# Mask on small PE tiles, norm turns on the full array, ten value moves for sixteen, and new engine orders in a fused attention stack

## The reference

```python
for i in range(DEPTH):                       # 6 layers
    x = attn_layer(shift_tokens(x), Wqkv[i], q_scale[i], k_scale[i], Wo[i]) + x
    x = ffn_layer(shift_tokens(x), ln_g[i], ln_b[i], W1[i], b1[i], W2[i], b2[i]) + x
# attn_layer: 16 heads of 64, windows of 32 tokens
q, k = l2norm(q) * qs, l2norm(k) * ksc       # then rotary with scales
mask = (it < jb) | (it > jb + w) | (jb == -1)    # a query sees 64 keys: its window and the one before
sim  = jnp.where(mask, -max, einsum('bhwie,bhwje->bhwij', bq, bk2) * QK_SCALE)
out  = einsum('bhwij,bhwje->bhwie', softmax(sim), bv2)   # then @ Wo
# ffn_layer: layer norm, a, gate = xn @ W1 + b1;  (a * gelu(gate)) @ W2 + b2
```

## Time and profile before

| | |
|---|---|
| median of 3 runs | 3445.39 us (3439.58 to 3446.2) |
| the profiled execution, by its own clock | 3448.65 us |
| its span, first to last instruction | 3446.9 us |
| mean granted TensorE clock | 0.991 of full speed |
| busy: PE, PEld, DVE, ACT, POOL | 3333.7, 2469.4, 2439.3, 2701.8, 1445.0 us |

### The profile page before, as it was taken

How to read it: one execution, slowest core, us unless ns; L and a number is a source line. 1 busy time by engine, 2 the same in 40 slices (tenths; PEclk the granted TensorE clock), 3 DMA queues, 4 the chain that set the end, 5 groups by cost and what they waited for, 6 DMA issues and landing times.

```text
span 3446.9 us, 152524 instructions
## 1 busy us (share of the span) xinstructions
PE 3333.7 (97%) x63228; PEld 2469.4 (72%) x63228; DVE 2439.3 (71%) x5141; ACT 2701.8 (78%) x9033; POOL 1445.0 (42%) x1276
## 2 busy tenths in 40 slices
PE   7789999999999999999999999999999999999997
PEld 4457777777777777777777777777777777777775
DVE  5667777777777777777777777777777767777773
ACT  5667887878787787878788787877878787887875
POOL 2244443444444354444444443453434444443441
PEclk9999999999999999999999999999999999999998
DMA  2056655665655666565565655565565656556563
GB/s 73 1 109 132 131 123 126 134 136 115 147 118 125 129 137 132 128 131 123 120 148 117 139 128 128 122 138 127 121 141 120 132 127 133 122 121 136 114 135 75
DMA packets 361274, 421.43 MB, mean 122 GB/s; under 512 B 52291, under 2 KB 265814, under 8 KB 359814
## 3 DMA queue, kind: packets, MB, share of 16 engines
q1 hardware_dynamic: 360582, 411.67, 55.2%
HBM read 19.30 MB, written 2.10 MB: 6 GB/s over the span
## 4 chain that ended last, share of the span: by engine, by line
PE 70%; POOL 18%; issue 4%; DVE 2%; ACT 1%; DMA 0%; SPq 0%; POOLq 0%; DVEq 0%
PE ring_ps L1234 16%; POOL qs L617 13%; PE out_ps L1326 12%; PE out_ps L1336 10%; PE ring_ps L1279 8%; PE small_ps L1245 6%; PE score_ps L1297 4%; PE ring_ps L1308 4%; PE ring_ps L1372 4%; POOL probs L601 3%; DVE prod L993 2%; PE ring_ps L1269 2%; PE out_ps L1350 2%; PE score_ps L1289 1%; PE small_ps L1253 1%
## 5 line engine op out<-in xcount | busy, mean ns | idle before, releaser
L774 ACT ACTIVATE probs<-score_ps,neg_max,rq 128x64 f32<-128x64 f32 x3072 | 1194.7, 420 | 95.7 <-DVE neg_max L1031 94.5
L993 DVE TENSOR_TENSOR prod<-ring_ps,tables 128x512 f32<-128x512 f32 x1536 | 956.9, 680 | 285.6 <-PE ring_ps L1234 257.8
L617 POOL TENSOR_TENSOR ks<-prod 128x1024 f32<-128x1024 f32 x192 | 452.7, 2358 | 852.5 <-DVE prod L993 852.4
L1234 PE MATMUL ring_ps<-xs,wqk 128*128 128x256 f32 x3072 | 768.9, 388 | 15.5 <-issue 10.6
L774 ACT ACTIVATION_READ_ACCUMULATOR probs<-score_ps,neg_max,rq 128x1 f32 x3072 | 677.1, 220 | 0.0
L730 ACT ACTIVATE square<-ring_ps,biases 128x512 f32<-128x512 f32 x768 | 516.9, 687 | 197.2 <-DVE prod L993 196.0
L1234 PEld LDWEIGHTS ring_ps<-xs,wqk 128*128 128x128 f32 x3072 | 571.1, 191 | 104.3 <-issue 17.6
L601 POOL TENSOR_TENSOR probs<-probs,inv_sums 128x512 f32<-128x512 f32 x384 | 401.1, 1045 | 576.0 <-DVE inv_sums L1045 576.0
L617 POOL TENSOR_TENSOR qs<-prod 128x1024 f32<-128x1024 f32 x192 | 453.4, 2361 | 395.4 <-DVE prod L993 395.4
L1326 PEld LDWEIGHTS out_ps<-pt,v 64*64 64x64 f32 x24576 | 397.0, 135 | 113.5 <-issue 111.6
L763 ACT ACTIVATE att_t<-out_ps 128x512 f32<-128x512 f32 x384 | 217.0, 591 | 297.3 <-PE out_ps L1326 297.2
(11 more groups left out here) (182 smaller groups left out, 3835.6 us busy)
## 6 DMA issues: line engine op xcount, KB each, us to landing
v<-vs SPq DMA_DIRECT2D x1344, 128.0 KB
qt<-qs SPq DMA_DIRECT2D x768, 128.0 KB
kt<-ks SPq DMA_DIRECT2D x768, 128.0 KB
v<-vs SPq DMA_DIRECT2D x192, 64.0 KB
wqk<-in_L_ffn_Wqkv SPq DMA_DIRECT2D x6, 1024.0 KB, 5.1
wv<-in_L_ffn_Wqkv SPq DMA_DIRECT2D x6, 512.0 KB, 5.8
wo<-in_L_ffn_Wo SPq DMA_DIRECT2D x6, 512.0 KB
out_dram<-ks SPq DMA_DIRECT2D x16, 128.0 KB, 1.9
```

The source lines that it names most:

```text
L617: pool.tensor_tensor(dst, prod_a[p % 2], prod_b[p % 2], ALU.add).then_inc(rot_ready, 1)
L774: last = nc.scalar.activation(probs[i][:, j, e, :], score_ps[e][:, KEYS * j:KEYS * (j + 1)], ACT.Exp, bias=neg_max[:, h:h + 1], scale=rq[p ...
L993: last = V.tensor_tensor((prod_b if a else prod_a)[p % 2][:, f, :] .rearrange("p (u c) -> p u c", u=2), bank[:, :].rearrange("p (u c) -> p ...
L1234: last = mm(bank_of(s)[:, TOKENS * f:TOKENS * (f + 1)], wqk[:, n, 2 * c + f, a, :], xs[:, WINDOW:PADDED], start=True, stop=True)
```

## The change

The mask is kept once for 32 queries (two copies, for the two halves of the partitions) with an extra row for the first window, and is added by eight matmuls on 64x32 tiles, each with a 64x32 selector as weights. The three bf16 parts of the key norms become eight, five of them zero, so that TU's output and KN's input fill 128 partitions. The `head_sel` table has 128 rows accordingly. `move_v` moves 64 partitions in one transfer where it moved 32 twice. All engine orders but SP's are new, PAD's place among the banks too.

```diff
-V_MOVES = 16
+RK_PARTS = P // HEADS
+V_MOVES = 10
...
 PE_ORDER = """
-PA0 PB0 PA1 S00 S01 PB1 BI WO PA2 NK CEN PB2 VAR PA3 PB3 TK UP0 UP1 S10 S11 V0 UP2 T00 TU NQ KN0 PAD V1 PV00 KN1
-TQ T01 V2 DN T10 PV01 V3 T11 PV10 PV11
+PA0 PB0 BI PAD S00 S01 PA1 PB1 PB2 WO NK PA2 CEN PB3 PA3 TK VAR S10 S11 UP0 UP1 T00 UP2 TU V1 KN0 KN1 NQ PV00
+T01 V3 DN V0 TQ PV01 T10 V2 T11 PV10 PV11
...
 DVE_ORDER = """
-XS RA0 RB0 RA1 M0 RB1 BI XA XB AR00 RA2 RB2 CK XG RB3 RA3 H0 M1 AR01 H1 TC00 UC H2 KM0 CQ VC1 KM1 AR10 TC01 X
-AR11 TC10 VC3 TC11
+XS RA0 RB0 M0 BI RB1 RA1 RB2 AR00 XA XB CK RA2 RB3 RA3 XG M1 H0 AR01 TC00 UC H1 H2 KM0 VC1 KM1 CQ TC01 VC3 X
+AR10 AR11 TC10 TC11
...
 ACT_ORDER = """
-QA0 QB0 QA1 E00 QB1 E01 E02 SQ QA2 LN E03 QB2 RTK LG G0 QB3 QA3 G1 VC0 G2 LE E10 E11 E12 E13 VC2 OC00 OC01 OC10
-RTQ OC11
+QA0 QB0 E00 E01 QB1 QA1 E02 QB2 E03 SQ QA2 LN RTK LG G0 QB3 QA3 G1 G2 LE E10 E11 E12 E13 VC0 OC00 OC01 RTQ VC2
+OC10 OC11
...
 POOL_ORDER = """
-AD0 AD1 AD2 AN00 AD3 RK TB0 AN01 TB1 AN10 TB2 AN11 TB3
+AD0 AD1 AN00 AD2 AD3 RK AN01 AN10 TB0 TB1 TB2 AN11 TB3
...
-        mask_bf = sb("mask_bf", [P, TILES, PAIRS, KEYS], BF16)
+        mask_bf = sb("mask_bf", [P, PAIRS, KEYS], BF16)
+        mask_sel_bf = sb("mask_sel_bf", [P, 2, WINDOW], BF16)
...
-        head_sel_bf = sb("head_sel_bf", [3 * HEADS, QUADS, P], BF16)
+        head_sel_bf = sb("head_sel_bf", [P, QUADS, P], BF16)
...
-        rk_bf = sb("rk_bf", [P, TILES, 3, HEADS], BF16)
-        rkt = sb("rkt", [3 * HEADS, TOKENS], BF16)
+        rk_bf = sb("rk_bf", [P, TILES, RK_PARTS, HEADS], BF16)
+        rkt = sb("rkt", [P, TOKENS], BF16)
...
             def move_v():
                 for e in range(2):
-                    for m in range(WPT):
-                        src = vs[WINDOW * m:WINDOW * (m + 1), :, e, :]
-                        for half in range(2):
-                            row_ = KEYS * e + WINDOW * half
-                            w0_ = m + 1 - half
-                            tiles = TILES if w0_ < WPT else TILES - 1
-                            sp.dma_start(v2[row_:row_ + WINDOW, w0_:w0_ + WPT * (tiles - 1) + 1:WPT, :],
-                                         src[:, 0:tiles, :]).then_inc(v_moved, 16)
+                    top, low = KEYS * e, KEYS * e + WINDOW
+                    for m in range(WPT - 1):
+                        sp.dma_start(v2[top:top + KEYS, m + 1::WPT, :], vs[WINDOW * m:WINDOW * m + KEYS, :, e, :]
+                                     ).then_inc(v_moved, 16)
+                    sp.dma_start(v2[low:low + WINDOW, 0::WPT, :], vs[0:WINDOW, :, e, :]).then_inc(v_moved, 16)
+                    sp.dma_start(v2[top:top + WINDOW, WPT, :], vs[P - WINDOW:P, 0, e, :]).then_inc(v_moved, 16)
...
+            pool.memset(rk_bf[:, :, :, :], 0.0)
...
-            for i in range(TILES):
-                for j in range(PAIRS):
-                    last = pool.tensor_copy(mask_bf[:, i, j, :], mask[:, i, :])
+            pool.tensor_copy(mask_sel_bf[:, :, :], mask_sel[:, :, :])
+            for j in range(PAIRS):
+                last = pool.tensor_copy(mask_bf[:, j, :], mask[:, :])
...
-                    turn = bank_of(("TU",))[0:3 * HEADS, 0:TOKENS // 2].bitcast(BF16)
+                    turn = bank_of(("TU",))[:, 0:TOKENS // 2].bitcast(BF16)
...
-                        for e in range(2):
-                            if e == 1 and i == 0:
-                                pe.wait_ge(q_moved, moved(g, 1))
-                            mm(score_ps[e][:, :], ident_bf[:, :], mask_bf[:, i, :, :].rearrange("p j c -> p (j c)"),
-                               start=True, stop=False, skip_group_check=True)
+                        for w in range(WPT):
+                            for e in range(2):
+                                if (w, e) == (WPT - 1, 1) and i == 0:
+                                    pe.wait_ge(q_moved, moved(g, 1))
+                                mm(score_ps[e][WINDOW * w:WINDOW * (w + 1), :],
+                                   mask_sel_bf[64 * e:64 * e + 64, int((i, w) == (0, 0)), :],
+                                   mask_bf[64 * e:64 * e + 64, :, :].rearrange("p j c -> p (j c)"),
+                                   start=True, stop=False, skip_group_check=True)
...
+    mask = np.zeros((2, 64, KEYS), np.float32)
+    mask[:, 0:WINDOW] = np.where((key > query + WINDOW) | (query > key), MASKED, 0.0)
+    mask[:, WINDOW] = np.where(key < WINDOW, MASKED, 0.0)
...
+    mask_sel[:, 0:WINDOW] = np.eye(WINDOW, dtype=np.float32)[:, None, :]
+    mask_sel[:, WINDOW, 1] = 1.0
```

More of the change, by code:

```diff
@@ L280, in build @@
         mod_a = carve(P, BATCH, 6)
-        mask = carve(P, TILES, KEYS)
-        head_sel = carve(3 * HEADS, QUADS, P)
+        mask = carve(P, KEYS)
+        mask_sel = carve(P, 2, WINDOW)
+        head_sel = carve(P, QUADS, P)
         wmod = carve(P, 6 * DIM)
@@ L439, in _ @@
             load_x(2)
-            for dst, src in ((mask[:, :, :], t["mask"]), (head_ones[:, :], t["head_ones"]),
+            for dst, src in ((mask[:, :], t["mask"]), (mask_sel[:, :, :], t["mask_sel"]), (head_ones[:, :], t["head_ones"]),
                              (head_sel[:, :, :], t["head_sel"]), (rotary[:, :, :], t["rotary"])):
@@ L545, in make_tables @@
                                    -1.0 if a else 1.0, ALU.mult, ALU.mult).then_inc(tables_ready, 1)
-            pool.wait_ge(consts_landed, 16 * 4)
+            pool.wait_ge(consts_landed, 16 * 5)
             pool.wait_ge(cond_landed, 16 * 4)
@@ L1257, in step @@
                     bank_free(g, s)
-                    turn = bank_of(s)[0:3 * HEADS, 0:TOKENS // 2].bitcast(BF16)
+                    turn = bank_of(s)[:, 0:TOKENS // 2].bitcast(BF16)
                     for i in range(TILES):
@@ L1401, in shape_constants @@
     rotary = np.stack([f.T for f in four], 1).astype(np.float32).reshape(P, 2, 2, TOKENS)
-    query = np.arange(P)[:, None] % WINDOW
+    query = np.arange(WINDOW)[:, None]
     key = np.arange(KEYS)[None, :]
-    hidden = (key > query + WINDOW) | (query > key)
-    mask = np.zeros((P, TILES, KEYS), np.float32)
-    for i in range(TILES):
-        no_window = (i == 0) & (np.arange(P)[:, None] < WINDOW) & (key < WINDOW)
-        mask[:, i] = np.where(hidden | no_window, MASKED, 0.0)
+    mask = np.zeros((2, 64, KEYS), np.float32)
+    mask[:, 0:WINDOW] = np.where((key > query + WINDOW) | (query > key), MASKED, 0.0)
+    mask[:, WINDOW] = np.where(key < WINDOW, MASKED, 0.0)
+    mask_sel = np.zeros((2, 64, 2, WINDOW), np.float32)
+    mask_sel[:, 0:WINDOW] = np.eye(WINDOW, dtype=np.float32)[:, None, :]
+    mask_sel[:, WINDOW, 1] = 1.0
     head_ones = np.zeros((P, WINDOW), np.float32)
-    head_sel = np.zeros((HEADS, QUADS, P), np.float32)
+    head_sel = np.zeros((RK_PARTS, HEADS, QUADS, P), np.float32)
     for r in range(4):
@@ L1413, in shape_constants @@
         for u in range(QUADS):
-            head_sel[4 * u + r, u, HALF * r:HALF * (r + 1)] = 1.0
-    return {"ident": np.eye(P, dtype=np.float32), "mask": mask, "head_ones": head_ones,
-            "head_sel": np.concatenate([head_sel] * 3), "rotary": rotary,
+            head_sel[0:3, 4 * u + r, u, HALF * r:HALF * (r + 1)] = 1.0
+    return {"ident": np.eye(P, dtype=np.float32), "mask": mask.reshape(P, KEYS), "mask_sel": mask_sel.reshape(P, 2, WINDOW), "head_ones": head_ones,
+            "head_sel": head_sel.reshape(P, QUADS, P), "rotary": rotary,
             "biases": np.tile(np.array([LN_EPS, 0.0], np.float32), (P, 1)),
```

## The result

The changed kernel takes 3495.52 us (median of 4 runs, 3492.42 to 3498.57) beside 3444.7 us for the kernel before (median of 4 runs): a ratio of 1.015, 95% interval 1.0133 to 1.0168. It is slower by about 51 us. The prediction said 3406 us and faster; it was wrong in sign, and the time lies outside its range.

A forecast was written before the change was run, and what follows sets the result against it. PE, 97% busy with 70% of the chain, bounds the kernel. 33.05 - 0.42 - 0.31 - 0.22 + 0.35 = 32.45 us a period: 57 us won, 18 lost at edges, 3406 us for the median; range 3358 to 3446.

The forecast's parts named there:

- Mask: Before each scores step: eight matmuls on 64x32 tiles stream at once, 0.22 us for 0.43; 0.42 us a period won.
- Rival 2: Mask matmuls of each S step: column tiles go one after another, 0.86 us for 0.22; time 3495; chance 0.07.
- Turns: TU, KN0, KN1 and V1 on PE: full-array steps save changes of shape, net 0.31 us a period.
- Rival 4: At the turns: nothing saved, KN's 0.1 us being the weights' wait for DVE's copy; period 32.76, time 3435; chance 0.09.
- New waits of UP0 and UP2, 0.35 us: PE at UP0 and UP2 waits for ACT's path; 0.35 us a period charged, ends 0.1 and 0.8.
- Rival 3: Whole period: no new wait binds and the edges cost 5 us; period 32.10, time 3360; chance 0.09.
- M0 now stands right after two products, which end just as the scores do; no cost: DVE's negation after S0's scores: at 3.7, so exponentials and squares end at 9.6, NK needing them at 9.7.
- rival 1: ACT's path from the first exponential on: new waits of 0.8 us, mask 0.38; period 33.22, time 3479; chance 0.17.
- E00: ACT's first exponential after S0's scores: 1.53 us after M0's start, so at 5.2 us of the walked period.
- Value moves: both ends are zero: SP's value moves: ten issues for sixteen, read by PV00 some 10 us later, so they shorten nothing: zero.
- 44 us of hiccups, "I leave those": Across the 95 periods: 0.47 us each on top of the undisturbed 33.05, 44 us in all, left as they are.
- Layer edges: Five times in the run, AN11 waits behind TB0 to TB2 and T11, PV11 behind it: 3.6 x 5 = 18 us lost.

The follow-up runs named there:

- the mended run: Changed kernel with one wait more: POOL starts AD0 only after DVE's first negation of the period; 3471.39 us, ratio 1.0052.
- the run with sixteen: Changed kernel with the sixteen value moves of before in place of the ten; 3463.48 us, ratio 1.0033.
- the run without the bytes: Changed kernel with its ten value moves cut to 8 KB each after the first batch, same number and place; 3450.26 us, ratio 1.0008.

## Why the prediction was wrong, by its own steps

- **Mask: right.** The eight matmuls take 0.22 us from their start to the scores (848.00 to 848.22): all eight tiles stream at once, as nearly as the rows can tell. The change of shape moved in front of it: the eight projections ahead of S0 take 1.93 us (846.07 to 848.00), where eight such instructions take 1.73 in the earlier trace rows. Rival 2 (column tiles one after another) did not happen; that its time, 3495, is the measured one is a coincidence. The rule of the Trainium skill that the prediction cited for it (TensorE: Matmul & The Clock Gate, Part 3) does not hold for these tiles, as the prediction read it: it gives 0.86 us for the 0.22.
- **Turns: right, within 0.05 us.** TU takes 0.11 us (866.44 to 866.55; 0.22 before), KN0 and KN1 together 0.53 (0.64 before), V1 0.92 (1.06 before). Rival 4 falls; that its period, 32.76, is the measured one is a coincidence too.
- **TU's wait: right.** 0.49 us from T00 to UP2 and no wait behind it.
- **New waits of UP0 and UP2, 0.35 us: wrong, they are none.** UP0's weights wait 18 us in the whole run, 0.2 us a period, hidden behind PE's running work. The wait for UP2 was a slip besides: 17.6 + 0.51 + 0.48 is 18.6, not 18.8, and PE is there at 18.7. With M0's wait mended the period is 32.02 us, 1.03 below 33.05; the other terms promised 0.95. Rival 3's 32.10 was the right size of what mask, turns and orders can give.
- **"M0 now stands right after two products, which end just as the scores do; no cost": the first step that failed.** The walk took M0's duration from a period in which POOL was idle beside it. The new order puts M0 beside AD0, the negation takes 0.86 us longer, and the walk had left NK 0.1 us of slack: that makes 0.76 us, and PE stands still there for 0.68. It is the place of rival 1 (ACT's path from E00 on), with a cause that the rival did not name; its size in the run is the 0.75 us that the mended run shows. The prediction charged 0.35 where there was nothing and nothing where there was 0.75, and so was only 0.32 us a period (30 us) off in sum.
- **"Value moves: both ends are zero": the second, and the largest.** The step asked only who waits for the moves' data, and there it was right: PV00 never did. It did not ask what else uses the DMA engines while ten moves of up to 256 KB fill them: 40 us by the run with sixteen, 49 by the run without the bytes.
- **44 us of hiccups, "I leave those": the third.** They were in large part PE's stops by issue (21 us of idle time in the 95 periods of the kernel before), and they are not fixed. In S0 the kernel before shows 4.0 us of them, the orders alone 13.5, mask and turns alone 16.8, both without the moves' bytes 19.2, with ten whole moves 41.2. Why orders and mask raise them was not settled. That S0 runs through 136 short instructions in 1.61 us (848.00 to 849.61), and that a block of instructions can hardly come sooner there, is only argued. In no run do two instruction packets start less than 3.2 us apart, which fits; but mask and turns alone shorten the stretch from the last PV step to the end of S0 only from 6.9 to 6.8 us (medians) and still have four times the idle time, so it can't be all.
- **Layer edges: right in mechanism, half in size.** T11's wait was predicted at 3.6 us and is 3.30; but PV is 1.37 and the projections 1.79 us longer behind it, at a lower clock. That makes 6.5 us an edge, and with the stop in S0 at the first edge 39 us on top in all, not 18.

The sum of the misses: 30 us in the period, 18 at the edges (39 us for the 3 of before and the 18 predicted), 44 in the stops elsewhere (85 for 41), less 4 outside: 3410 + 88 = 3498 for an execution like the profiled one, which took 3498.57.

## What to carry to other kernels

When steps are reordered, a duration read from the old trace holds only with the old neighbours: look at what each moved instruction will stand beside, its ports and its queue included. A transfer that nobody waits for still costs if it fills the DMA engines while the matrix engine needs its next instructions; start it behind the densest stretch, and prefer gaps in PE that stay short. And a long stop of PE is often charged twice, once for itself and once for the slower clock behind it, so the hiccups of a trace are a term of the sum like any other.

## What the runs showed of the hardware that was not expected

- A DVE instruction of 0.17 us took 1.03, up to the very end of POOL's instruction, where both read SBUF.
- Every stop of PE by issue in S0, in all the runs, ends 1.2 to 2.0 us after an instruction packet has ended. Moves between partitions that keep the DMA engines 0.98 busy go with stops of up to 4.2 us in that dense step; with 8 KB moves in their place none in it was over 2.1 us.
- A stop of 1.55 us left the next twelve projections at 2.86 us; one of 3.16 us made them 5.49, at a granted clock of 0.50. Yet one of 1.78 us in another run was followed by 0.50, and one of 3.27 us by 1.00.
- Eight bf16 matmuls of 512 columns on 64x32 tiles take 0.22 us together, as long as one on the full array by the prediction's estimate.
